# Combining a block's last tiles on VectorE in aligned pairs, with gate and base operations 1024 columns wide

## The chip, the cores and the metric

The kernel runs on one core of one Trainium2 chip, in float32. The metric is the device time of one execution in microseconds; lower is better.

## The reference, cut to what matters

The block is an adaLN transformer layer: a first half (RWKV-like time and channel mixing) gives `x4`, and a second half is a mixture of experts on it. What the change touches is the last sum:

```
h   = layernorm(x4) * (1 + cb) + sb
out = x4 + gb * (shared(h) + sum over the top 2 of 16 experts of gate_e * expert_e(h))
```

`x4` is 4 batches of 512 tokens with 512 channels. In the kernel that is 16 tiles of 128 tokens by 512 channels, tiles 0 to 3 being batch 0 and so on. `gb` is one row of 512 numbers per batch.

## The kernel before, in words

The routed experts are computed on tokens sorted by expert: a loop over pairs of slots of 128 tokens on TensorE, ScalarE and VectorE, whose results SP stores in `ys_s` in HBM. It ends about 875 us into the span. This document is about the 55 us behind it.

**What the work behind the loop is.** For each of the 16 tiles the final sum is put together in `g1b[:, t]` in SBUF:

1. GpSimd gathers the tile's rows of `ys_s`, first those of the lower expert into `g1b` (line 2567), then those of the upper into `g2b` (line 2574). These are indirect DMAs; the row numbers are in `spos` in SBUF. The order is: lower 0 to 9, upper 0 to 7, lower 10 to 15, a wait for the first up-projection of batch 3 (`s_up`), upper 8 to 15. The gather of an upper tile t from 8 on also waits until t - 7 tiles are counted in `s_o4`.
2. ScalarE scales `g1b[:, t]` by the lower gate (`scaled`, line 2350).
3. VectorE adds the upper part times its gate (`upper_row`, line 1939).
4. From tile 8 on, the shared expert's down-projection lies in PSUM, and VectorE adds it (`shared_row`, line 1944) and counts `s_gsh`.
5. VectorE multiplies by `gb` (`gated`, line 1948).
6. Tiles 0 to 7 and 12 to 15: VectorE adds a base, `base8` or `bsb` (`based`, line 1954), and counts `s_o4`; SP waits for each tile's count in turn and stores it to the output (line 853). Tiles 8 to 11 have no base operation: `s_o4` is counted behind the gate, and GpSimd adds them onto the output with an accumulating DMA (line 2597), where `x4` lies already.

**What runs beside it.** TensorE computes the shared expert for batches 2 and 3 in parts of 128 mid-channels, 4 to a batch. The up-projection of part n (8 to 11 for batch 2, 12 to 15 for batch 3) writes `up_ps[n % 2]`; ScalarE applies Gelu (line 2290) and copies the high part out (line 2298); VectorE subtracts it to get the low part (`mid_lo(n)`, line 1743). The up-projection of part n waits for `mid_lo(n - 2)`, which frees the bank. The down-projections take `mid_lo` of all four parts. `ht_lo(3, ...)` (line 1737) makes the low parts of batch 3's input.

**What sets the order.** Each engine's order is written out by hand. On VectorE it is the list at the end of its program: `mid_lo` and `ht_lo` calls with `combine` calls between them. `combine` takes a list of one or two tiles and does each step for all of them before the next step; an operation waits (`s_dve` or `s_gsh`) only for the one of its own tile, so that in a pair the other tile's operation runs between the two.

Of the kernel before, what the change touches and what calls it, by code (L numbers as in the profile page):

```python
# [17 lines left out]
ALU = mybir.AluOpType  # L18
# [3 lines left out]
P = 128  # L22
H = 512
# [3 lines left out]
TT = T // P  # L27
# [14 lines left out]
SB = 2  # L42
ERING = RING - BASE
NG = 8
LATE = (NB - 1) * TT
# [21 lines left out]
def adaln_block(nc, x_d, c_d, wmod_d, vecs_d, wtm_d, wcm_d, wrt_d, wex_d, out_d):  # L67
    top = ExitStack()
    with top:
        def sem(name):  # L70
            return top.enter_context(nc.semaphore(name))

        def sbuf(stack, name, shape, dt=F32):
            return stack.enter_context(nc.sbuf_tensor(name, shape, dt))
# [109 lines left out]
        g1b = sbuf(overlay, "g1b", [P, NT, H])  # L184
# [11 lines left out]
        bsb = sbuf(overlay, "bsb", [P, NT - LATE, H])  # L196
# [26 lines left out]
        base8 = sbuf(ph3, "base8", [P, SB * TT, H])  # L223
# [12 lines left out]
        now = sbuf(ph3, "now", [P, NE])  # L236
# [26 lines left out]
        gb2 = sbuf(ph4, "gb2", [P, NB, H])  # L263
# [61 lines left out]
        s_dve = sem("s_dve")  # L325
# [10 lines left out]
        s_gsh = sem("s_gsh")  # L336
# [31 lines left out]
        s_o4 = sem("s_o4")  # L368
# [97 lines left out]
        def gathered(t):  # L466

            i = t % NG
            before = 32 * NB if i < TT else 0 if i < TT + 2 else 16 * (NE - PRE) // 2
            return before + 16 * (t // NG + 1)  # L470
# [13 lines left out]
        def dn_of(t):  # L484
            return dn_ps[t % 4] if t < SB * TT else dn5_ps[(t - SB * TT) % 6]
# [777 lines left out]
        def _(dve):  # L1263
            own = Count(s_dve)
# [433 lines left out]
            for g in range(NB * MF):  # L1698
                b, m = divmod(g, MF)
                t = (b - 1) * TT  # L1700
# [30 lines left out]
            def ht_lo(b, tiles):  # L1731
                if 0 in tiles:
                    dve.wait_ge(s_htlo, b * KT)
                hi, lo = (ht_of(b)[:, i] for i in range(2))
                for k in tiles:
                    dve.wait_ge(s_hthi, b * KT + k + 1)
                    dve.tensor_tensor(lo[:, k, :], lo[:, k, :].bitcast(F32), hi[:, k, :].bitcast(F32), ALU.subtract)\
                        .then_inc(s_htlo, 1)

            def mid_lo(n):  # L1740
                b, m = divmod(n, KT)
                dve.wait_ge(s_midhi, n + 1)
                dve.tensor_tensor(mid_of(b)[:, 1, m, :], up_ps[n % 2][:, :], mid_of(b)[:, 0, m, :].bitcast(F32),
                                  ALU.subtract).then_inc(s_midlo, 1)
# [101 lines left out]
            t = NT - TT  # L1846
# [87 lines left out]
            def upper_row(t):  # L1934
                dve.wait_ge(s_o1, t + 1)
                dve.wait_ge(s_gat[t % NG], gathered(t))
                if t == 0:
                    dve.wait_ge(s_gates, 1)
                return own.up(dve.scalar_tensor_tensor(out=g1b[:, t], in0=g2b[:, t], scalar=gates[:, 1, t:t + 1],
                                                       in1=g1b[:, t], op0=ALU.mult, op1=ALU.add))  # L1940

            def shared_row(t):
                dve.wait_ge(s_dn, t + 1)
                dve.tensor_tensor(g1b[:, t], dn_of(t)[:, :], g1b[:, t], ALU.add).then_inc(s_gsh, 1)

            def gated(t):
                dve.wait_ge(s_bsl, 16 * (NT - LATE + NB))
                return dve.tensor_tensor(g1b[:, t], g1b[:, t], gb2[:, t // TT], ALU.mult)

            def based(t):  # L1950
                if t == 0:
                    dve.wait_ge(s_base, 16 * SB * TT)
                base = base8[:, t] if t < SB * TT else bsb[:, t - LATE]
                dve.tensor_tensor(g1b[:, t], g1b[:, t], base, ALU.add).then_inc(s_o4, 1)

            def combine(tiles, middle=()):
                now = {}
                for t in tiles:
                    now[t] = upper_row(t)
                for n in middle:  # L1960
                    mid_lo(n)
                if tiles[0] >= SB * TT:
                    for t in tiles:
                        dve.wait_ge(s_dve, now[t])
                        shared_row(t)
                for t in tiles:
                    if t >= SB * TT:
                        dve.wait_ge(s_gsh, t + 1)
                    else:
                        dve.wait_ge(s_dve, now[t])  # L1970
                    if SB * TT <= t < LATE:
                        gated(t).then_inc(s_o4, 1)
                        del now[t]
                        continue
                    now[t] = own.up(gated(t))
                for t in tiles:
                    if t in now:
                        dve.wait_ge(s_dve, now[t])
                        based(t)

            mid_lo(8)
            mid_lo(9)
            combine([0])
            mid_lo(10)
            ht_lo(3, [0, 1])
            mid_lo(11)
            ht_lo(3, [2, 3])
            combine([1, 2])
            combine([3, 4])
            combine([5, 6])  # L1990
            mid_lo(12)
            combine([7])
            mid_lo(13)
            combine([8, 9], middle=[14])
            mid_lo(15)
            combine([10, 11])
            combine([12, 13])
            combine([14, 15])

        @block.scalar  # L2000
        def _(act):
# [635 lines left out]
```

## Time and profile before

| what | value |
|---|---|
| runs of the kernel | 936.26 us median of 3 (936.14 to 937.33) |
| the profiled execution | 932.21 us, span 930.4 us |
| granted TensorE clock, mean | 0.99 of full |
| TensorE busy over the span | 887.3 us (95%) |
| VectorE busy over the span | 523.6 us (56%) |
| ScalarE, GpSimd busy | 383.0 us (41%), 387.1 us (42%) |

The span is what the trace covers of the execution. Durations in the rows come from this one execution; `xN` is the number of instructions in a group, and an arrow `<-` behind an idle time names what ended it.

### The profile page before, as it was taken

Reading aid. Unit: us, or ns where it says so; the run is one execution under the profiler, and the core shown is the slowest. Engines: PE = TensorE matmul, PEld = TensorE weight load, DVE = VectorE, ACT = ScalarE, POOL = GpSimd, SP = SyncE. Lnnn points to the kernel's source line nnn. Section 1 sums busy time; section 2 is a strip of 40 time slices with the busy share of each in tenths; the row PEclk is TensorE's granted clock in tenths of the full one; section 3 lists DMA queues with packets and bytes.
Section 4 is the critical chain, followed back from the end, with each engine's and each line's share of the span. In section 5 each row is a group of like instructions: output and inputs, shape, how many; then the busy total and the mean of one; then the engine's idle time right before and its main releaser. Section 6 shows DMA issues by size and latency. Waiting matters only on the chain.

```text
span 930.4 us, 13567 instructions
## 1 busy us (share of the span) xinstructions
PE 887.3 (95%) x4264; PEld 714.8 (77%) x4265; DVE 523.6 (56%) x999; ACT 383.0 (41%) x632; POOL 387.1 (42%) x282
## 2 busy tenths in 40 slices
PE   6899879999998999999999999999999999999995
PEld 2467658878776888888888888888887888878874
DVE  5798797998667111263226522651496444444388
ACT  2666565583735533322232223225443333333252
POOL 3331200100022546316301630268537699888584
PEclk9999989999999999999999999999999999999998
DMA  9657578566056327487213421466435789786787
GB/s 354 214 150 230 198 234 264 162 201 215 1 171 218 131 93 237 145 261 260 91 35 129 143 91 35 137 216 225 159 115 183 243 259 275 270 270 204 248 245 173
DMA packets 121824, 174.03 MB, mean 187 GB/s; under 512 B 8216, under 2 KB 69656, under 8 KB 118704
## 3 DMA queue, kind: packets, MB, share of 16 engines
q1 hardware_dynamic: 58896, 111.55, 35.4%
q0 software_dynamic: 9216, 34.61, 12.1%
q10 hardware_dynamic: 53664, 27.26, 10.4%
q8 instruction: 27, 0.44, 0.2%
q14 instruction: 21, 0.17, 0.1%
HBM read 97.58 MB, written 75.81 MB: 186 GB/s over the span
## 4 chain that ended last, share of the span: by engine, by line
PE 76%; DVE 7%; DMA 5%; POOL 4%; issue 4%; ACT 2%; SPq 0%; DVEq 0%; ACTq 0%; POOLq 0%
PE kk_ps L426 6%; PE kv_ps L426 6%; PE kk_ps L428 6%; PE kv_ps L428 6%; PE kk_ps L427 6%; PE kv_ps L427 6%; PE mm_ps L426 6%; PE mm_ps L428 6%; PE mm_ps L427 6%; PE up_ps L426 3%; POOL g1b L2567 2%; DMA xsb<-xs_s 2%; PE up_ps L427 2%; PE up_ps L428 2%; PE dn_ps L428 2%
## 5 line engine op out<-in xcount | busy, mean ns | idle before, releaser
L1569 DVE TENSOR_TENSOR silu<-kk_ps,silu 128x512 fp32r<-128x512 f32 x64 | 44.3, 692 | 198.5 <-ACT silu L2238 197.9
L2234 ACT ACTIVATE kk_ps<-kk_ps 128x512 f32<-128x512 f32 x64 | 37.2, 582 | 207.2 <-PE kk_ps L428 207.2
L426 PE MATMUL kk_ps<-xk,cm_w 128*128 128x512 f32 x256 | 100.8, 394 | 0.0
L426 PE MATMUL kv_ps<-cm_w,silu 128*128 128x512 f32 x256 | 100.5, 393 | 0.0
L428 PE MATMUL kk_ps<-xk,cm_w 128*128 128x512 f32 x256 | 99.8, 390 | 0.0
L428 PE MATMUL kv_ps<-cm_w,silu 128*128 128x512 f32 x256 | 99.7, 390 | 0.0
L427 PE MATMUL kk_ps<-xk,cm_w 128*128 128x512 f32 x256 | 99.6, 389 | 0.0
L427 PE MATMUL kv_ps<-cm_w,silu 128*128 128x512 f32 x256 | 99.6, 389 | 0.0
L2404 POOL TENSOR_TENSOR cm_w<-stage,cm_w 128x1024 fp32r<-128x1024 f32 x16 | 38.7, 2426 | 88.3 <-ACT cm_w L2019 72.5
L1896 DVE TENSOR_TENSOR xsT<-xs_ps,xsT 128x512 fp32r<-128x512 f32 x42 | 29.1, 692 | 75.7 <-ACT xsT L2321 75.6
L2411 POOL TENSOR_TENSOR rs<-mv,neghalf 128x4 f32<-128x4 f32 (+2 forms) x13 | 13.5, 1039 | 133.8 <-DVE mv L1279 133.7
L2462 POOL TENSOR_TENSOR rs<-mv,neghalf 128x1 f32<-128x1 f32 x16 | 16.1, 1009 | 126.4 <-DVE mv L1594 126.4
L2047 ACT ACTIVATE mix<-raw_ps 128x512 fp32r<-128x512 f32 x64 | 37.4, 594 | 56.7 <-DVE raw_ps L1350 54.0
L426 PE MATMUL mm_ps<-mix,wkv_w 128*128 128x512 f32 x128 | 52.4, 409 | 5.0 <-DVE x2b L1391 4.1
L428 PEld LDWEIGHTS kv_ps<-cm_w,silu 128*128 128x128 f32 x256 | 48.1, 188 | 10.2
L428 PEld LDWEIGHTS kk_ps<-xk,cm_w 128*128 128x128 f32 x256 | 48.0, 188 | 10.2
L427 PEld LDWEIGHTS kv_ps<-cm_w,silu 128*128 128x128 f32 x256 | 48.1, 188 | 9.8
L427 PEld LDWEIGHTS kk_ps<-xk,cm_w 128*128 128x128 f32 x256 | 48.1, 188 | 9.7
L426 PEld LDWEIGHTS kv_ps<-cm_w,silu 128*128 128x128 f32 x256 | 48.1, 188 | 9.7
L426 PEld LDWEIGHTS kk_ps<-xk,cm_w 128*128 128x128 f32 x256 | 48.1, 188 | 9.6
L1350 DVE SCALAR_TENSOR_TENSOR raw_ps<-dT,vecs,hT 128x512 f32<-128x512 f32 x64 | 49.9, 796 | 3.0
L427 PE MATMUL mm_ps<-mix,wkv_w 128*128 128x512 f32 x128 | 50.6, 396 | 0.0
(298 smaller groups left out, 2338.5 us busy)
## 6 DMA issues: line engine op xcount, KB each, us to landing
xs_s<-zero ACTq DMA_DIRECT2D x13, 1024.0 KB, 6.2
ys_s<-zero ACTq DMA_DIRECT2D x13, 1024.0 KB, 6.4
xsb<-xs_s SPq DMA_DIRECT2D x44, 256.0 KB, 3.4
ys_s<-ysb SPq DMA_DIRECT2D x41, 256.0 KB, 3.6
ex_raw<-in_wex POOLq DMA_DIRECT2D x9, 1024.0 KB, 6.7
stage<-in_wcm SPq DMA_DIRECT2D x16, 512.0 KB, 4.0
wmod<-in_wmod SPq DMA_DIRECT2D x6, 1024.0 KB, 12.2
ex_raw<-in_wex SPq DMA_DIRECT2D x6, 1024.0 KB, 7.7
```

The costliest lines, as they stand in the source:

```text
L426: pe.matmul(out, lhs[0], rhs[0], start=first, stop=False)
L427: pe.matmul(out, lhs[0], rhs[1], start=False, stop=False)
L428: return pe.matmul(out, lhs[1], rhs[0], start=False, stop=last)
L1350: dve.scalar_tensor_tensor(out=out, in0=dT[:, k, :], scalar=vecs[:, vec, k:k + 1], in1=hT[:, k, 0:T], op0=ALU.mult, op1=ALU.add).then_inc( ...
L1569: dve.tensor_tensor(silu[:, g % NSILU, 1, :], kk_ps[g % 2][:, :], silu[:, g % NSILU, 0, :].bitcast(F32), ALU.subtract).then_inc(s_silo, 1)
L1896: dve.tensor_tensor(xsT[:, par, 1], xs_ps[par][:, :, :], xsT[:, par, 0].bitcast(F32), ALU.subtract)\
L2047: act.activation(mix[:, i % 2, 0, k, :], raw_at(s, b, k), ACT.Copy)\
L2234: act.activation(kk_ps[g % 2][:, :], kk_ps[g % 2][:, :], ACT.Silu).then_inc(s_silu, 1)
L2404: pool.tensor_tensor(w[:, 1, k0:k0 + KT // 2, :], stage[:, n % 2].rearrange("p (k c) -> p k c", c=H), w[:, 0, k0:k0 + KT // 2, :].bitcast( ...
L2411: pool.tensor_tensor(rs[:, j0:j1].rearrange("p (t a) -> p t a", a=1), mv[:, j0:j1, 1:2], neghalf[:, :].rearrange("p (t a) -> p t a", a=1). ...
L2462: pool.tensor_tensor(rs5[:, t % 2:t % 2 + 1], mv5[:, t % 2, 1:2], neghalf[:, :], ALU.pow)\
L2567: pool.indirect_dma_start(g1b[:, t], None, ys_s, bass.IndirectOffsetOnAxis(ap=spos[:, 0, t:t + 1], axis=0))\
```

## The change

Four edits, all in VectorE's program. `combine(t)` now takes an even tile number and treats tiles t and t + 1. `gated` and `based` work on both tiles in one instruction of 1024 columns, the gate row being read twice by a broadcast. They can start only when the operations before them are through for both tiles, and they count `s_o4` by 2 at once. `shared_row` and `upper_row` stay one instruction per tile. The pairs are 0-1, 2-3, ... 14-15 in place of 0, 1-2, 3-4, 5-6, 7, 8-9, ...: tile 0, which stood between `mid_lo(9)` and `mid_lo(10)`, moves behind `mid_lo(11)` and `ht_lo(3, [2, 3])`, and tile 7 stands before `mid_lo(13)` together with tile 6.

```diff
             def gated(t):
                 dve.wait_ge(s_bsl, 16 * (NT - LATE + NB))
-                return dve.tensor_tensor(g1b[:, t], g1b[:, t], gb2[:, t // TT], ALU.mult)
+                b = t // TT
+                return dve.tensor_tensor(g1b[:, t:t + 2], g1b[:, t:t + 2],
+                                         gb2[:, b:b + 1].to_broadcast([P, 2, H]), ALU.mult)
 
             def based(t):
                 if t == 0:
                     dve.wait_ge(s_base, 16 * SB * TT)
-                base = base8[:, t] if t < SB * TT else bsb[:, t - LATE]
-                dve.tensor_tensor(g1b[:, t], g1b[:, t], base, ALU.add).then_inc(s_o4, 1)
-
-            def combine(tiles, middle=()):
-                now = {}
-                for t in tiles:
-                    now[t] = upper_row(t)
+                base = base8[:, t:t + 2] if t < SB * TT else bsb[:, t - LATE:t - LATE + 2]
+                dve.tensor_tensor(g1b[:, t:t + 2], g1b[:, t:t + 2], base, ALU.add).then_inc(s_o4, 2)
+
+            def combine(t, middle=()):
+
+                now = [upper_row(t), upper_row(t + 1)]
                 for n in middle:
                     mid_lo(n)
-                if tiles[0] >= SB * TT:
-                    for t in tiles:
-                        dve.wait_ge(s_dve, now[t])
-                        shared_row(t)
-                for t in tiles:
-                    if t >= SB * TT:
-                        dve.wait_ge(s_gsh, t + 1)
-                    else:
-                        dve.wait_ge(s_dve, now[t])
-                    if SB * TT <= t < LATE:
-                        gated(t).then_inc(s_o4, 1)
-                        del now[t]
-                        continue
-                    now[t] = own.up(gated(t))
-                for t in tiles:
-                    if t in now:
-                        dve.wait_ge(s_dve, now[t])
-                        based(t)
+                if t >= SB * TT:
+                    for i in range(2):
+                        dve.wait_ge(s_dve, now[i])
+                        shared_row(t + i)
+                    dve.wait_ge(s_gsh, t + 2)
+                else:
+                    dve.wait_ge(s_dve, now[1])
+                if SB * TT <= t < LATE:
+                    gated(t).then_inc(s_o4, 2)
+                else:
+                    dve.wait_ge(s_dve, own.up(gated(t)))
+                    based(t)
 
             mid_lo(8)
             mid_lo(9)
-            combine([0])
             mid_lo(10)
             ht_lo(3, [0, 1])
             mid_lo(11)
             ht_lo(3, [2, 3])
-            combine([1, 2])
-            combine([3, 4])
-            combine([5, 6])
+            combine(0)
+            combine(2)
+            combine(4)
             mid_lo(12)
-            combine([7])
+            combine(6)
             mid_lo(13)
-            combine([8, 9], middle=[14])
+            combine(8, middle=[14])
             mid_lo(15)
-            combine([10, 11])
-            combine([12, 13])
-            combine([14, 15])
+            combine(10)
+            combine(12)
+            combine(14)
```

## Rows read from the trace of the kernel before

**Rows 1.** Chain that ended last, 860 to 931 us: start us, us, what

```profile
900.00 3.43 POOL g1b L2567
...
903.73 0.96 POOL g2b L2574
...
905.00 4.91 DMA g2b<-ys_s,spos
```

**Rows 2.** VectorE in order of time, first tile and first pair: start us, us, engine, line

```profile
884.73 0.75 DVE L1939 SCALAR_TENSOR_TENSOR g1b<-g2b,gates,g1b 128x512 f32<-128x512 f32 x1 [3.31 <-DMA g2b<-ys_s,spos]
885.51 0.69 DVE L1948 TENSOR_TENSOR g1b<-g1b,gb 128x512 f32<-128x512 f32 x1
886.24 0.69 DVE L1954 TENSOR_TENSOR g1b<-g1b,base 128x512 f32<-128x512 f32 x1
886.85 0.68 DVE L1743 TENSOR_TENSOR mid<-up_ps,mid 128x512 fp32r<-128x512 f32 x1
...
891.31 1.41 DVE L1939 SCALAR_TENSOR_TENSOR g1b<-g2b,gates,g1b 128x512 f32<-128x512 f32 x2
892.63 1.29 DVE L1948 TENSOR_TENSOR g1b<-g1b,gb 128x512 f32<-128x512 f32 x2
893.84 1.29 DVE L1954 TENSOR_TENSOR g1b<-g1b,base 128x512 f32<-128x512 f32 x2
895.04 1.41 DVE L1939 SCALAR_TENSOR_TENSOR g1b<-g2b,gates,g1b 128x512 f32<-128x512 f32 x2
```

**Rows 3.** VectorE in order of time, the middle of the stretch

```profile
902.51 0.69 DVE L1743 TENSOR_TENSOR ht<-up_ps,ht 128x512 fp32r<-128x512 f32 x1
...
905.23 0.68 DVE L1743 TENSOR_TENSOR ht<-up_ps,ht 128x512 fp32r<-128x512 f32 x1
907.86 0.75 DVE L1939 SCALAR_TENSOR_TENSOR g1b<-g2b,gates,g1b 128x512 f32<-128x512 f32 x1 [1.94 <-DMA g2b<-ys_s,spos]
910.00 0.75 DVE L1939 SCALAR_TENSOR_TENSOR g1b<-g2b,gates,g1b 128x512 f32<-128x512 f32 x1 [1.39 <-DMA g2b<-ys_s,spos]
910.67 0.68 DVE L1743 TENSOR_TENSOR ht<-up_ps,ht 128x512 fp32r<-128x512 f32 x1
```

**Rows 4.** VectorE in order of time, the last three pairs

```profile
914.27 1.41 DVE L1939 SCALAR_TENSOR_TENSOR g1b<-g2b,gates,g1b 128x512 f32<-128x512 f32 x2
...
917.99 1.41 DVE L1939 SCALAR_TENSOR_TENSOR g1b<-g2b,gates,g1b 128x512 f32<-128x512 f32 x2
...
926.64 1.29 DVE L1954 TENSOR_TENSOR g1b<-g1b,bsb 128x512 f32<-128x512 f32 x2
```

**Rows 5.** GpSimd in order of time, two of the lower gathers

```profile
893.86 1.50 POOL L2567 DMA_INDIRECT g1b<-ys_s,spos  x1 [0.30 <-issue]
...
896.93 2.76 POOL L2567 DMA_INDIRECT g1b<-ys_s,spos  x1 [0.30 <-issue]
```

**Rows 6.** VectorE groups by line, two widths: xcount | busy us, mean ns | idle before

```profile
L1896 DVE TENSOR_TENSOR xsT<-xs_ps,xsT 128x512 fp32r<-128x512 f32 x42 | 29.1, 692 | 75.7 <-ACT xsT L2321 75.6
...
L1901 DVE TENSOR_TENSOR mbT<-tm_ps,mbT 128x256 fp32r<-128x256 f32 x41 | 17.2, 419 | 0.2 <-DVE base L1755 0.2
```

**Rows 7.** ScalarE in order of time, the last batch's activations

```profile
900.26 0.58 ACT L2290 ACTIVATE up_ps<-up_ps 128x512 f32<-128x512 f32 x1 [5.89 <-PE up_ps L428]
...
906.35 0.58 ACT L2290 ACTIVATE up_ps<-up_ps 128x512 f32<-128x512 f32 x1 [2.16 <-PE up_ps L428]
```

**Rows 8.** TensorE in order of time, first product of an up-projection tile

```profile
903.25 0.50 PE L426 MATMUL up_ps<-mid,ex_w 128*128 128x512 f32 x1 [0.31 <-DVE ht L1743]
```

**Rows 9.** Busy time by stretch: us, PE, PEld, DVE, ACT, POOL, clock, DMA share, GB/s

```profile
922.00:924.00 2.00, 0.00 (x0) 0.00 (x0) 2.00 (x4) 0.00 (x0) 0.00 (x0) 1.00 0.93 217
```

**Rows 10.** SP's queue in order of time, two loads issued back to back

```profile
567.92 0.92 SPq L629 DMA_DIRECT2D xkr<-xk_s  x2
```

**Rows 11.** Line 853, SP's output stores: issue ns, first and last start, landing

```profile
L853 SPq DMA_DIRECT2D out<-g1b x12: 332/332/342, 887.0 to 928.0; - x12
...
DMA to landing us min/median/max: 2.0/2.6/4.8
```

## The prediction, made before the changed kernel was run

> **What bounds the kernel now.** I read the chain of waits first, from its end. The reader is to see that behind the experts' loop it runs along GpSimd's queue of gathers, through one lower gather of 3.43 us, into the upper gathers of tiles 8 and 9, the second of which lands 4.91 us after its issue [rows 1]. Then I read VectorE in order of time. It works without a gap from 891.31 to about 905.9, then stands 1.94 us for tile 8's gather and 1.39 us for tile 9's [rows 3], 3.33 us in all, and from 910.00 runs without a gap to 926.64 + 1.29 = 927.93 us [rows 4]. TensorE has nothing left from 922 us on [rows 9], so it does not set the end. After VectorE only the store of tile 15 is left: it is issued at 928.0 and takes at least 2.0 us to land [rows 11], and the span ends at 930.4. So what counts is when VectorE's last operation ends.
>
> **Part 1, tile 0 moves.** Its three operations and the start of part 10 take 884.73 to 886.85 = 2.12 us, in a stretch where VectorE otherwise idles (3.31 us before it) [rows 2]. They move behind 891.31, into the gapless run: 2.12 us more before the waits for tiles 8 and 9. The low part of part 10 can start only 0.1 us sooner, as ScalarE's copy is its other input; nothing gained there. SP's store of tile 0 goes with it, from 887 to about 895 us; nothing but other stores stands behind it in SP's queue. No gather waits for tile 0 so early: the first, tile 8's, starts at 903.73.
>
> **Part 2, two operations become one.** Two independent 512-column operations of one line are 893.84 - 892.63 = 1.21 us apart [rows 2], 0.60 each. The trace has no 1024-column operation on VectorE. From below I bound it by the slope between 256 and 512 columns: 692 - 419 = 273 ns [rows 6], so 692 + 546 = 1.24 us long and 0.60 + 0.55 = 1.15 us to the next independent start; from above by 1.21, no gain at all. I take 1.15, as the slope is of the same kind of instruction. By the Trainium skill ("VectorE: DVE Perf Modes", section on the TRN2 errata) an fp32 tensor_tensor takes (N + 151) / 0.96 ns, 1224 ns at 1024; over 14 operations that would make the sum 0.2 us smaller.
>
> **Part 3, the waits inside a pair.** An operation that waits for the one just before it starts 886.24 - 885.51 = 0.73 us after it, against 0.60: 0.13 us of latency, and 0.78 behind an upper operation, against 0.66 [rows 2]. In the old pairs the other tile's operation covered this. Now the gate waits for the second upper or shared operation, and the base for the whole gate. So, start to start:
> - pairs of tiles 0 to 7: 0.66 + 0.78 + (0.73 + 0.55) + 1.15 = 3.87 us, before 895.04 - 891.31 = 3.73 [rows 2];
> - a pair with a shared part and no base (8, 10): 1.32 + 0.60 + 0.73 + 1.15 = 3.80 us, before 917.99 - 914.27 = 3.72 [rows 4];
> - a pair with both (12, 14): 1.32 + 0.60 + 0.73 + 1.28 + 1.15 = 5.08 us, before (927.93 - 917.99) / 2 less the last one's tail of 0.04 = 4.93 [rows 4].
> By itself the pairing costs 0.14, 0.08 and 0.15 us a pair; the wide operation does not pay for its wait.
>
> **Part 4, the gathers.** A gather on GpSimd normally takes 0.96 us [rows 1], but some take 1.50, 2.76 and 3.43 [rows 1, 5]. Lined up with VectorE by what they take over 0.96: the one at 893.86 seems held until 894.40, 0.56 us after a base of two SBUF inputs began [rows 2]; the one at 896.93 until 898.73, 0.04 before the next pair begins (895.04 + 3.73); the one at 900.00 until 902.47, 0.04 before a low part, which has a PSUM input [rows 3]. So a gather that starts beside gates and bases waits until one ends, and can miss the gap of about 0.05 us to the next, several times in a row. After the change the gap before each gate and each base is some 0.13 us wider, by part 3. I take it that a gather gets in there, so that one wide operation at most holds it: 1.1 us. Lined up so, the six lower gathers end at about 899 to 901 us, not 903.43. The upper gathers then wait for the first up-projection of batch 3, which ScalarE sees at 900.26 [rows 7], so tile 8's starts between 900.3 and 901.5 and tile 9's by 903.0, landing by 908. The Trainium skill ("SBUF — State Buffer", section "Who interferes with whom") says that a VectorE instruction with two SBUF inputs contends with a GpSimd instruction that reads SBUF, and that the second one waits for the whole of the first. The rows agree for these gathers; that it speaks against wider operations is a rival below.
>
> **The sum.** From 891.31, three pairs: 891.31 + 3 x 3.87 = 902.92; part 12's low part 903.52; pair 6: 907.39, so part 13 starts there and not at 905.23 [rows 3]; 907.99 tiles 8 and 9, now ready: 909.31; part 14: 909.91; shared 0.60 + 0.73: 911.24; gate: 912.39. Part 15's low part needs TensorE, which waits for part 13's: 907.39 + 0.69 = 908.1. From a held start at 903.25 [rows 8] ScalarE's Gelu followed at 906.35 [rows 7], 3.10 us; the low part comes two activations later, 0.62 + 0.63: 908.1 + 3.10 + 1.25 = 912.45, so a wait of 0.06. Then 913.05, pair 10: 916.85, pair 12: 921.93, pair 14 with its tail of 0.09: 927.10, against 927.93: 0.83 us less. In short: the waits for tiles 8 and 9 go, 3.53 us from start to start (891.31 + 3 x 3.73 + 2.12 + 1.20 + 1.32 = 907.14 would be part 14's start, and it is 910.67); tiles 0 to 7 take 4 x 3.87 = 15.48 us in the run in place of 13.31, so 2.17 more; 2 x 0.08 + 2 x 0.15 + 0.06 are paid behind: 0.83 left.
> At the end both stores of the last pair are released together. Before, tile 14's went 0.6 us ahead. Two issues on SP take 0.92 us, 0.46 each [rows 10], so tile 15's goes 0.46 us later than it could: 0.83 - 0.46 = **0.4 us faster**. The profiled execution's 932.21 becomes 931.8; the median stands 4.05 us above it, so 935.9.
> What hides the rest: TensorE's part 15 comes 2 us later, but its last down-projection, with 0.6 us of this passed on, is done by 922.6, and its reader stands at about 923.9. If that cover went, TensorE would add up to 1 us. GpSimd's accumulating stores of tiles 10 and 11 start where pair 10's gate ends, 0.3 us earlier.
>
> **The rivals.** 0.2% is 1.9 us, about what a measurement of this kernel can tell from no change.
> - *A, forecast, 0.48*: 935.9.
> - *B, gathers as late as before, 0.27*: GpSimd still misses gaps. Tile 9's gather lands at 909.9 and its operation starts at 910.00. The end gains nothing and pays 2 x 0.08 + 2 x 0.15 + 0.46: +0.9 us, 937.2. For it: the 2.76 and 3.43. Against it: gaps about three times as wide.
> - *C, slower, 0.11*: the hold grows. Gathers get in only where a run of two-SBUF operations ends. Pair 6 now runs from 903.5 to 907.4, right over tile 8's and 9's gathers, where before only tile 7 stood. If tile 8's starts at 903.73 and is held to 907.2, it needs 0.96 us more and some 3 to land, 911.2, and tile 9's follows 1.3 us later at 912.5: 2.5 us later than 910.0, and 0.9 paid: 939.7. It decides from the point where tile 9's gather lands after 911. By the Trainium skill's rule above a hold is one instruction, here 1.24 us; it takes a run of them to reach this price.
> - *D, faster, 0.07*: the 0.13 us waits are not there for wide operations. Thirteen of them lie on the way, two in each pair from 0 to 6 (part 15 moves with them) and five behind part 15; 13 x 0.13 = 1.7 us: 934.2.
> - *E, it does not do what it says, 0.07*: the broadcast read makes the gate slower than two operations (up to 2 x 0.69 = 1.38 us, 0.23 more, eight times: +1.8), or the time moves for reasons outside of this stretch: 934 to 938.
>
> **How the numbers follow.** The likeliest is A. A and B hold 0.75; C lies above and D below. From 934.5 to 937.8 takes in A, B, the bound of no gain per wide operation (14 x 0.06 = 0.8 us) and most of E. Faster by over 1.9 us (below 934.4): D and a part of E, 0.10. Slower by over 1.9 us (above 938.1): C and a little of E, 0.13. Within: 0.77.
>
> **What would show it.** Wide gates and bases of 1.22 to 1.24 us; 1.27 us from a gate to its base; no idle time on VectorE before tiles 8 and 9; lower gathers 13 to 15 under 2.1 us each; tile 8's upper gather at 900.3 to 901.5; VectorE's end near 927.1 and two stores 0.46 us apart. A wait for tile 9's gather of over 1 us proves A wrong; a wide operation over 1.3 us proves part 2 wrong; a last TensorE product after 923 proves the cover wrong.

## The result, and the profile after

The changed kernel takes 942.52 us (median of 6, 940.69 to 947.66), the kernel before 936.80 in the same session (median of 6, 935.05 to 941.43). The ratio is 1.006, 95% interval 1.0037 to 1.0083: slower, by 5.7 us between the medians. The forecast of 935.9 and its range up to 937.8 both missed. In a later session one execution of a version below took 1785.94 us and one of the kernel before 1457.24; the ratios leave them out.

The profiled execution took 942.66 us, its span is 940.9. VectorE in order of time, from the copy that frees the loop's last bank to the end of the run of pairs (start us, us, engine, line, what; in brackets the idle time before and what ended it):

```profile
885.73 0.69 DVE L1909 COPY ysb<-dn_ps 128x512 f32<-128x512 f32 x1 [5.03 <-remote]
...
896.97 1.41 DVE L1939 SCALAR_TENSOR_TENSOR g1b<-g2b,gates,g1b 128x512 f32<-128x512 f32 x2
898.41 1.22 DVE L1949 TENSOR_TENSOR g1b<-g1b,gb 128x1024 f32<-128x1024 f32 x1
899.72 1.23 DVE L1956 TENSOR_TENSOR g1b<-g1b,base 128x1024 f32<-128x1024 f32 x1
900.87 1.41 DVE L1939 SCALAR_TENSOR_TENSOR g1b<-g2b,gates,g1b 128x512 f32<-128x512 f32 x2
...
907.55 1.23 DVE L1956 TENSOR_TENSOR g1b<-g1b,base 128x1024 f32<-128x1024 f32 x1
913.43 0.69 DVE L1743 TENSOR_TENSOR ht<-up_ps,ht 128x512 fp32r<-128x512 f32 x1 [4.66 <-ACT ht L2292]
...
923.63 1.41 DVE L1939 SCALAR_TENSOR_TENSOR g1b<-g2b,gates,g1b 128x512 f32<-128x512 f32 x2
...
927.47 1.41 DVE L1939 SCALAR_TENSOR_TENSOR g1b<-g2b,gates,g1b 128x512 f32<-128x512 f32 x2
...
932.59 1.41 DVE L1939 SCALAR_TENSOR_TENSOR g1b<-g2b,gates,g1b 128x512 f32<-128x512 f32 x2
...
936.56 1.23 DVE L1956 TENSOR_TENSOR g1b<-g1b,bsb 128x1024 f32<-128x1024 f32 x1
```

Everything that VectorE does by itself came as worked out: wide operations of 1.22 to 1.23 us, 1.31 us from a gate to its base (forecast 1.28), 3.90 us for a pair of tiles 0 to 7 (3.87), 3.84 for pair 10 (3.80), 5.12 for pair 12 (5.08). The waits for tiles 8 and 9 of [rows 3] are gone. In their place stands one wait, 4.66 us, for part 12's low part, which the forecast had without a wait.

GpSimd, lower gathers from tile 10 on and the first upper one:

```profile
899.51 0.96 POOL L2561 DMA_INDIRECT g1b<-ys_s,spos  x1 [0.30 <-issue]
900.78 1.00 POOL L2561 DMA_INDIRECT g1b<-ys_s,spos  x1 [0.30 <-issue]
...
906.01 1.01 POOL L2561 DMA_INDIRECT g1b<-ys_s,spos  x1 [0.32 <-issue]
912.42 0.96 POOL L2568 DMA_INDIRECT g2b<-ys_s,spos  x1 [5.40 <-PE up_ps L428]
```

None is held now, against 1.50, 2.76 and 3.43 us [rows 1, 5]. But tile 8's upper gather waits 5.40 us, for the same thing as VectorE: part 12's up-projection. TensorE and ScalarE there:

```profile
904.50 0.39 PE L426 MATMUL up_ps<-mid,ex_w 128*128 128x512 f32 x1
904.84 0.40 PE L427 MATMUL up_ps<-mid,ex_w 128*128 128x512 f32 x1
906.97 0.39 PE L428 MATMUL up_ps<-mid,ex_w 128*128 128x512 f32 x1 [1.73 <-issue]
908.40 0.39 PE L426 MATMUL up_ps<-mid,ex_w 128*128 128x512 f32 x1 [1.05 <-issue]
...
910.67 0.63 PE L426 MATMUL up_ps<-mid,ex_w 128*128 128x512 f32 x1
...
911.52 0.63 PE L428 MATMUL up_ps<-mid,ex_w 128*128 128x512 f32 x1
```

```profile
912.19 0.58 ACT L2284 ACTIVATE up_ps<-up_ps 128x512 f32<-128x512 f32 x1 [12.15 <-PE up_ps L428]
```

TensorE stands between products of part 12's one up-projection, for 1.73, 1.05 and, before the next product, 0.32 us, waiting for nothing that the profile shows ("issue"). Behind this half-idle stretch the granted clock is lower (mean 0.60 over 909 to 913 us, so partly at 1.2 GHz, with products 0.43 us apart in place of 0.23). Twelve products 0.23 us apart from 904.50 would end at about 907.4; they end at 911.52 + 0.63 = 912.15. By an estimate from these rows, 3.7 of the 4.8 us are the stops and 1.1 the lower clock. ScalarE starts at once behind them, so in this trace VectorE's 4.66 us are TensorE's own lateness. The first row of VectorE above, its 5.03 us of idle time at the loop's exit, is not in the trace read for the forecast, but it is no work of the change: the kernel before shows it too, as the first experiment tells.

### The profile page after: what moved, and what is told of

It is laid out like the page before. It is cut to its first block, busy times and chain, and to the rows that moved or that the text cites. A ratio compares the mean times of both kernels' runs of the same rounds, so it can differ in the third digit from the quotient of the medians.

```text
span 940.9 us, 13550 instructions
## 1 busy us (share of the span) xinstructions
PE 893.0 (95%) x4264; PEld 718.3 (76%) x4265; DVE 523.8 (56%) x985; ACT 382.8 (41%) x632; POOL 381.9 (41%) x282
## 4 chain that ended last, share of the span: by engine, by line
PE 79%; DVE 8%; DMA 5%; issue 4%; ACT 3%; SPq 1%; POOL 1%; DVEq 0%; ACTq 0%
PE kk_ps L426 6%; PE kv_ps L426 6%; PE kk_ps L428 6%; PE kv_ps L428 6%; PE kk_ps L427 6%; PE kv_ps L427 6%; PE up_ps L426 4%; PE mm_ps L426 4%; PE mm_ps L427 4%; PE mm_ps L428 4%; PE up_ps L428 4%; PE up_ps L427 3%; PE dn_ps L426 3%; PE dn_ps L428 3%; PE dn_ps L427 3%
## 5 line engine op out<-in xcount | busy, mean ns | idle before, releaser
L428 PEld LDWEIGHTS kk_ps<-xk,cm_w 128*128 128x128 f32 x256 | 48.0, 188 | 10.2
```

The source lines that it names most:

```text
L428: return pe.matmul(out, lhs[1], rhs[0], start=False, stop=last)
```

## The experiments

Fourteen runs were made, of ten new kernels and four repeats. One number serves for all traces: the **run**, from the start of the first pair's upper operations (896.97 here) to the end of VectorE's last operation (936.56 + 1.23). For each trace I take VectorE's waits of 0.36 us or more in it off; the rest is work. (In the old order tile 0's operations stand ahead of the run, in the new one inside it.) The column "trace" is the time of the profiled execution. Ratios are to runs of the kernel before on the same chip. (These rows are worked out from VectorE's rows in order of time.)

```
kernel                        ratio  [95%]             run    waits   work   trace
before, as forecast from      -                        36.62   3.33   33.29   932.21
before, again                 1.0018 [0.9999, 1.0037]  34.57   1.18   33.39   936.45
wide 8-15, old order          1.0029 [1.0009, 1.0050]  35.36   1.33   34.03   935.80
wide all, old order           1.0029 [1.0010, 1.0049]  36.93   2.42   34.51   938.26
before, pauses                1.0028 [1.0011, 1.0046]  40.76   7.45   33.31   945.79
before, exit paused           1.0070 [1.0042, 1.0099]  39.81   6.44   33.37   940.50
new order, 512 wide           1.0044 [1.0026, 1.0062]  41.08   6.07   35.01   941.57
new order, 512 wide, again    1.0054 [1.0033, 1.0075]  40.29   5.25   35.04   941.09
after                         1.0060 [1.0037, 1.0083]  40.82   4.66   36.16   942.66
after, again                  1.0056 [1.0034, 1.0079]  43.87   7.47   36.40   943.73
after, stores late            1.0057 [1.0033, 1.0081]  43.10   6.88   36.22   941.12
after, gathers "spaced"       1.0051 [1.0029, 1.0072]  43.09   6.79   36.30   946.04
after, part 13 inside         1.0051 [1.0033, 1.0068]  40.85   4.75   36.10   940.96
after, pauses                 1.0018 [0.9995, 1.0040]  37.67   1.56   36.11   933.46
after, pauses + part 13       0.9981 [0.9959, 1.0003]  37.41   1.42   35.99   933.41
after, pauses + part 13 again 1.0016 [0.9995, 1.0037]  37.76   1.68   36.08   939.99
```

The control, text for text the kernel before, came out at 1.0018, and one text measured twice at 0.9981 and 1.0016. So differences below about 0.3% are not read. A trace is one execution: those of "before, pauses" and of the "spaced" version are the slowest of their twelve, those of "after, pauses" and of "wide 8-15" the fastest.

**Both kernels again.** No edit.

> The kernel before, unchanged, for a second trace and as a control of the comparison. Both theories: ratio 1.000 +- 0.002. Theory I: no issue stall of TensorE over 1 us between the loop's exit and the end, its last program fetch lies 1.5 us or more ahead of the product that needs it. Theory D: stalls of this kind show here too in some executions.

> The changed kernel once more. In its first trace VectorE's own operations behaved as forecast, and the time was lost in two places that the change does not touch: around the loop's exit (876 to 886 us) and where TensorE stood 1.7 + 1.0 + 0.3 us for instructions at 905 to 909 us, just as the last 16 KB piece of its program was fetched (906.0 us, against 895.8 before). Theory I (code fetch): the stall at TensorE's last fetch belongs to the changed kernel and comes back, with the product before it held 2 us or more; the ratio stays near 1.006 (1.004 to 1.008). Theory D (a disturbed trace): the lost time around the exit is chance of the loop and its transfers; the trace shows neither stall, and the ratio lies within 0.998 to 1.003.

Measured: 936.87 and 942.03 us. The difference is real and repeats. Neither theory on the stop of TensorE comes true as it stands. In the changed kernel's first trace the one 16 KB packet of the instruction queue in this stretch starts at 906.01 us and takes 0.91, and TensorE goes on at 906.97; that fits the first stop and not the two behind it. In the second trace the packet starts at 900.93, no product is held near it, and the ratio is the same. The kernel before's second trace is the more useful one. VectorE at the loop's exit, at tile 0, at the first pair, at part 12's low part and at tiles 8 and 9:

```profile
885.00 0.69 DVE L1909 COPY ysb<-dn_ps 128x512 f32<-128x512 f32 x1 [5.01 <-remote]
...
891.75 0.75 DVE L1939 SCALAR_TENSOR_TENSOR g1b<-g2b,gates,g1b 128x512 f32<-128x512 f32 x1 [3.72 <-DMA g2b<-ys_s,spos]
...
897.60 1.40 DVE L1939 SCALAR_TENSOR_TENSOR g1b<-g2b,gates,g1b 128x512 f32<-128x512 f32 x2
...
909.74 0.69 DVE L1743 TENSOR_TENSOR ht<-up_ps,ht 128x512 fp32r<-128x512 f32 x1 [0.74 <-issue]
...
913.59 1.42 DVE L1939 SCALAR_TENSOR_TENSOR g1b<-g2b,gates,g1b 128x512 f32<-128x512 f32 x2 [0.44 <-DMA g2b<-ys_s,spos]
```

Its six lower gathers take 0.96 us each, the first and the last of them:

```profile
898.88 0.96 POOL L2567 DMA_INDIRECT g1b<-ys_s,spos  x1 [0.30 <-issue]
...
905.21 0.96 POOL L2567 DMA_INDIRECT g1b<-ys_s,spos  x1 [0.30 <-issue]
```

Nothing holds them, and the wait for tiles 8 and 9 is 0.44 us, not 3.33. The exit's idle time, 5 to 6 us, stands in 12 of the 16 traces of the table, of either order. That the exit costs 5 us and the gathers are unheld in the one, and the reverse in the other, is how these two executions of one kernel differ (the trace of "before, pauses" has both); the forecast was made from the second kind, whose 932.21 us lie 4 us under the median.

In the changed kernel's second trace, TensorE is not late but its counts are:

```profile
910.79 0.39 PE L428 MATMUL up_ps<-mid,ex_w 128*128 128x512 f32 x1
917.34 0.80 PE L426 MATMUL up_ps<-mid,ex_w 128*128 128x512 f32 x1 [6.17 <-issue]
```

```profile
915.35 0.58 ACT L2284 ACTIVATE up_ps<-up_ps 128x512 f32<-128x512 f32 x1 [7.97 <-remote]
...
918.99 0.58 ACT L2284 ACTIVATE up_ps<-up_ps 128x512 f32<-128x512 f32 x1 [2.43 <-remote]
```

Part 13's last product ends at 908.2 and part 14's at 911.2; ScalarE, which has nothing else to do there, starts at 915.35 and 918.99, 7.2 and 7.8 us later. VectorE's low part of part 13 follows at 916.60, after 4.58 us of waiting, and TensorE's part 15 at 917.34: its 6.17 us, put down to "issue", are the wait for that low part.

**Order and width apart.** The pairs of the new order with operations of 512 columns, measured in two sessions; and the reverse, wide operations in the old order:

```diff
-            combine([0])
...
+            combine([0, 1])
+            combine([2, 3])
+            combine([4, 5])
             mid_lo(12)
-            combine([7])
+            combine([6, 7])
```

> Only the order of the change: tile 0 behind the low part 11, pairs 0-1 to 14-15, but every gate and base 512 columns wide and waiting for its own tile alone, as before. If the order does it (tile 0's move and both stores of a pair together beside TensorE's fetch and the gathers), the time is that of the changed kernel, 1.004 to 1.008 of before. If it is the wide operations, 0.998 to 1.001: by the sum made before, the order alone gives VectorE's end 0.3 to 1.0 us back.

> The order of the change with operations of 512 columns, a second time, for another trace. Its first trace had three gathers held 2.77, 3.42 and 3.43 us in a row, tile 8's upper gather issued 16.2 us behind the first pair (12.4 in the kernel before), and VectorE waiting 5.61 us for it. Theory H (hold): this comes again, three holds of over 2.5 us, a wait of over 4.5 us, ratio 1.003 to 1.006. Else the wait is under 3.5 us and the slowness has another place.

```diff
-            combine([8, 9], middle=[14])
+            combine_w(8, middle=[14])
...
-            combine([10, 11])
-            combine([12, 13])
-            combine([14, 15])
+            combine_w(10)
+            combine_w(12)
+            combine_w(14)
```

(`combine_w` is the changed kernel's `combine`; the second version has it for 1-2, 3-4 and 5-6 as well.)

> Only the wide operations, and only in the pairs that both kernels have (8-9, 10-11, 12-13, 14-15); tiles 0 to 7 in the old order and width. By the terms of the prediction: 2 x 0.08 + 2 x 0.15 for the waits and 0.46 for the late store, so 0.9 us slower, ratio 1.001. If the wide operations cause the loss by the program's length (6 VectorE instructions fewer) or in another way, 1.004 or more; if the order does, 1.001 or less.

> The wide operations everywhere (pairs 1-2, 3-4, 5-6, 8-9 and on), but tile 0 early and tile 7 alone as in the kernel before, so the order is the old one. If the wide operations free the gathers and that costs, the stall is here too: ratio 1.003 to 1.006. If it is tile 0's move and the pairing of the stores by two more tiles, 1.000 to 1.002 (prediction's terms: 3 x 0.14 + 0.9 us).

Measured: order alone 1.0044 and 1.0054, width alone 1.0029 twice. The order carries most of the loss; whether width costs anything stays open (both intervals lie above 1, but the control's 1.0018 is as near). With 512-wide operations in the new order ScalarE starts parts 12 to 14 within 0.1 us of each end, but GpSimd is held:

```profile
898.10 2.77 POOL L2573 DMA_INDIRECT g2b<-ys_s,spos  x1 [0.30 <-issue]
901.17 3.42 POOL L2566 DMA_INDIRECT g1b<-ys_s,spos  x1 [0.30 <-issue]
904.90 3.43 POOL L2566 DMA_INDIRECT g1b<-ys_s,spos  x1 [0.30 <-issue]
```

and VectorE pays for it at tile 8:

```profile
918.71 1.42 DVE L1939 SCALAR_TENSOR_TENSOR g1b<-g2b,gates,g1b 128x512 f32<-128x512 f32 x2 [5.61 <-DMA g2b<-ys_s,spos]
```

That is rival C's mechanism, held gathers in a longer run of pairs. C was priced at 3.4 us; the two ratios are 4.1 and 5.1 us. In the changed kernel the wide operations' waits do let the gathers in, as part 4 said; its loss has the same size by another way.

**Stores out of the way.** SP keeps tiles 0 to 7 back until eight are counted.

```diff
-                sp.wait_ge(s_o4, t + 1)
+                sp.wait_ge(s_o4, max(t + 1, SB * TT))
```

> The changed kernel, but SP stores tiles 0 to 7 only once all eight are counted (about 12 us later for the first). Theory S (saturation): once VectorE no longer holds the gathers, 14 to 22 of them run without a gap beside the pairs' stores, together 340 to 380 KB a us for 8 us, and in that stretch counts and instructions of the engines come late (TensorE's product held 3.5 and 6.2 us in the two traces, ScalarE 8 us behind TensorE's count). Without the stores in that stretch the stall shrinks under 1.5 us and the time falls by 2 to 5 us, ratio 0.999 to 1.003. Theory G: the gathers alone do it (there is a like stall at the loop's exit): unchanged, 1.004 or more.

Measured 943.6 us, 1.0057. ScalarE still starts parts 13 and 14 3.7 and 8.1 us late (ends 906.34 and 909.05):

```profile
910.04 0.58 ACT L2284 ACTIVATE up_ps<-up_ps 128x512 f32<-128x512 f32 x1 [5.17 <-PE up_ps L428]
...
917.15 0.58 ACT L2284 ACTIVATE up_ps<-up_ps 128x512 f32<-128x512 f32 x1 [5.90 <-remote]
```

No store is issued before 909.53, so the first lateness has none beside it, and the loss is what it was: the stores are not needed for it. Of the second this can't be said, as the held stores go out then.

**Gathers spaced.** Two waits for `s_o4` (2 and 4) before lower gathers 12 and 14.

> The changed kernel, but GpSimd issues the lower gathers 12 and 14 only when 2 and 4 tiles are counted, which puts gaps of 1 to 2 us where VectorE's holds had put them before. Theory S and theory G both: the stall behind the first pair shrinks under 1.5 us, ratio 0.999 to 1.003. A rival, that the time is lost by the wide operations or the order themselves: 1.005 as before.

Measured 941.46 us, 1.0051. The counts were already there when GpSimd came to the waits, so nothing was spaced and the trace is that of the changed kernel: ScalarE 6.5 and 7.8 us late (ends 911.26, 914.25; starts 917.77, 922.05). As a test of the gathers it is void; it is one more measurement of the changed kernel.

**Gathers paused,** with waits that hold:

```diff
             for t in range(SOON, NT):
+                if t == SOON + 3:
+                    pool.wait_ge(s_o4, 4)
                 gather_lower(t)
             pool.wait_ge(s_up, (NB - 1) * KT + 1)
+            pool.wait_ge(s_o4, 6)
```

> The changed kernel, but GpSimd waits for 4 counted tiles ahead of lower gather 13 and for 6 ahead of tile 8's upper gather, so that the 14 to 24 gathers in a row get two real pauses (the waits of f2_gathers_spaced were over before they were reached, so it spaced nothing). Theory G: in traces where over about 14 gathers ran without a pause TensorE's counts reached ScalarE late (7.1 and 7.8 us in e1_after_again, 3.7 and 8.0 in f1_stores_late); with the pauses each up-projection's count arrives within 0.5 us, VectorE has no wait over 1 us before part 12 and 13, and the ratio is 0.998 to 1.003. Theory O (order): the low part of part 13 behind a whole pair costs by itself: late counts or not, ratio 1.004 or more.

Measured 936.83 us, 1.0018: most of the loss is gone. The pause, and ScalarE on time:

```profile
899.08 1.22 POOL L2561 DMA_INDIRECT g1b<-ys_s,spos  x1 [3.35 <-DVE g1b L1956]
```

```profile
902.51 0.58 ACT L2284 ACTIVATE up_ps<-up_ps 128x512 f32<-128x512 f32 x1 [1.50 <-PE up_ps L428]
```

The end of each up-projection and ScalarE's start are within 0.1 us (902.5 and 902.51, 906.4 and 906.44). What is left is 1.56 us for tile 8's gather, and 1.50 us in which TensorE's part 15 waits for part 13's low part, which stands behind pair 6.

**Part 13's low part inside pair 6,** with the pauses, twice, and without them:

```diff
-            combine(6)
-            mid_lo(13)
+            combine(6, middle=[13])
```

> f5_gathers_paused, and the low part of part 13 in the middle of pair 6 instead of behind it, 2.5 us sooner, so that TensorE's part 15 isn't held. Theory O: TensorE's gap before part 15 (1.4 us at the least with the new order, none in the kernel before) goes, and the time falls by 1 to 3 us below f5. Theory G alone: within 0.5 us of f5, as TensorE has the slack; ratio 0.998 to 1.002.

> The changed kernel with both edits (two pauses in the gathers, part 13's low part inside pair 6), the same text as before, to narrow the interval: 934.2 to 935.5, 0.998 to 0.9995 of the kernel before if the gain is real; 1.000 to 1.001 if the first result was a lucky draw.

> The changed kernel with one edit: part 13's low part stands inside pair 6, behind its two upper operations, and no pause is put into GpSimd's gathers. Theory 'cover' (a low part behind a whole pair leaves TensorE's part 15 late; worth 1.9 to 2.6 us): 939 to 940.5, and with the late counts and the wait for part 12's low part left as they are, still 1.003 to 1.004 of the kernel before. Rival 'pauses' (the unbroken row of gathers is all of it): 941.5 to 942.5, 1.005 to 1.006, and ScalarE still starts part 13 over 3 us behind the end of its up-projection. If both are worth something, the two edits together (934.25 in an earlier run) minus the pauses alone (936.8) give 2.6 us for this edit, and the pauses the other 5.

Measured: 934.25 us (0.9981) and 939.48 us (1.0016) with the pauses, 940.96 us (1.0051) without. TensorE's gap before part 15 is gone in all three, but the time is not the better for it where the counts or issues are late: alone the edit gives nothing that can be told from the changed kernel. By the ratio that speaks for the expectation's rival, "pauses"; by the time it lies between the two, and that rival's sign, ScalarE over 3 us late at part 13, isn't in the trace. There TensorE stops within part 12 instead, as in the changed kernel's first trace:

```profile
905.72 0.49 PE L426 MATMUL up_ps<-mid,ex_w 128*128 128x512 f32 x1 [1.03 <-issue]
```

(The 16 KB packet of the instruction queue comes 3 us behind it, at 908.68.) In one session, with part 13 inside in both, the pauses bring the ratio from 1.0051 to 1.0016; the intervals just overlap. On top of the pauses its effect can't be told apart either, as the same text differs by as much from session to session. The second trace with the pauses has the loop exit's stall (4.99 us) and still a short run (37.76), so the pauses' effect on the run does not hang on that stall being absent.

**The kernel before, paused.** The same two pauses, at counts 5 and 7; and another, GpSimd waiting for the loop's end behind the fourth early gather, to keep the exit free.

> The kernel before with the two pauses alone (lower gather 13 behind tile 4's base, tile 8's upper gather behind tile 6's). If pauses help by themselves, whatever the pairing, then 934 to 935.5 (0.998 to 0.999), and the pairing would be worth nothing in the kernel with both edits. If they only mend what the change brings, 936 to 937.5 (0.9995 to 1.001): this kernel paused for 2.5 to 3.5 us by itself, and the later start of tile 8's upper gather (902.5 for 903.7) leaves the wait for tile 9's at its 1.4 us.

> The kernel before, but GpSimd pauses behind its fourth lower gather until the loop's last stores have landed. Its second trace had TensorE standing 2.8 us at the loop's exit and VectorE 5.0 us for the last slot, with 10 gathers in a row beside. Theory G (a long row of gathers makes counts and loop transfers late) : the exit has no gap over 1 us, the loop's last copy comes within 1 us of its product. The gathers end 4 to 6 us later themselves, so the time is about the same or some us worse, ratio 0.998 to 1.006. If the exit's gap stays at 2.8 us, it isn't the gathers.

Measured: 940.02 us (1.0028) and 941.07 us (1.007). Neither helps. In the first, three gathers in a row are held for 3.44, 3.43 and 3.42 us, and VectorE waits 6.85 us for ScalarE's scaled tile 8; the two pauses add nothing to that in this trace, since GpSimd reaches them late (0.30 us before each gather, as without them). So this trace, the slowest of its twelve, doesn't show a paused kernel at all, and the ratio can't be told from the control's. In the second the exit's stall is gone, but so it is in three other traces without this pause, which settles nothing. The later gathers cost: tile 0's operations wait 8.92 us and part 10's low part stands behind them, and in the run VectorE waits 2.18 us for part 12's low part and 4.26 for the gathers of tiles 8 and 9. So no gain from pauses is seen in the old order; in the new one they mend what it brings. No version was found that is measurably faster than the kernel before.

## Why the prediction was wrong

- **Parts 2 and 3, the cost of pairing: right.** The work of the run rose from 33.29 and 33.39 us to between 35.99 and 36.40, 2.6 to 3.1 more; the sum had 2.17 + 2 x 0.08 + 2 x 0.15 = 2.63. By the formula in the Trainium skill ("VectorE: DVE Perf Modes", section on the TRN2 errata) 1024 columns take 1.224 us, and the trace agrees with 1.22 to 1.23; the slope's 1.24 was 0.02 too long.
- **Part 1, tile 0: nearly right.** It cost its 2 us. "Nothing gained there" was wrong for executions in which tile 0's gather is late: there it held up part 10's low part. From the exit's copy to the first pair is 897.60 - 885.00 = 12.60 us before and 896.97 - 885.73 = 11.24 after, 1.36 less in these two traces.
- **Part 4, the gathers get in: right,** 0.96 to 1.02 us each. In none of the nine traces with wide operations on tiles 0 to 7 does one take over 1.78 us; with 512 columns one of 2.76 or more is in five of seven. But the kernel before can have them free too, and **what that was worth was wrong: the credit of 3.53 us** for the waits for tiles 8 and 9. In the kernel before's second trace these waits are 0.44 us. The forecast took the stall of one execution for the kernel's, though its own 4.05 us between that execution and the median said that it was not a usual one.
- **The sum's path through the low parts failed.** It runs from 902.92 to 903.52 and from 907.39 to 907.99 without a wait, so it takes it that ScalarE is done with parts 12 and 13 when VectorE comes to them, and books 0.06 us for part 15's. Part 12's low part waited 4.66 us; in the repeat the four low parts waited 0.59, 4.58, 1.63 and 0.67. No term stood for stops within TensorE's own work or for its counts being late. The sign given for this path failed with it: tile 8's upper gather starts 15.5 us behind the first pair, not 9.0 to 10.2. The cover that "What hides the rest" asks for, TensorE's last down-projection ahead of its reader, held by itself: the last product ends at 932.24 + 0.39 = 932.63 us and tile 15's shared operation starts at about 934.5.

```profile
932.24 0.39 PE L428 MATMUL dn_ps<-ex_w,ht 128*128 128x512 f32 x1
```

```profile
933.91 1.28 DVE L1944 TENSOR_TENSOR g1b<-dn_ps,g1b 128x512 f32<-128x512 f32 x2
```

- **In part 4, the rule that the gathers were said to agree with was read too widely.** In the Trainium skill ("SBUF — State Buffer", section "Who interferes with whom") a wait for the whole of one instruction is spelled out for VectorE's 2-port modes, and the same section has it that a tensor_tensor was not seen to stall a DMA. The rows here show gathers held beside such operations, and for more than one of them.

Together, from the exit's copy to VectorE's end, the second trace of before against the trace of after: 52.06 - 47.17 = 4.89 us, which is -1.36 in front of the run, +2.77 of work, +3.48 of waits (4.66 - 1.18). Behind VectorE's end the span goes on for 3.1 us, in both traces of before for 2.5: the two stores released together, 0.6 where 0.46 was forecast. With the pauses the same kernel has 1.4 to 1.7 us of waits, and comes out at 1.0018, 0.9981 and 1.0016: added work alone is 2.77 - 1.36 + 0.6 = 2.0 us, about what can be told from no change, and the waits make the rest. ("After, pauses" was read in its fastest execution; the 1.68 us of the repeat with part 13 inside are from a usual one.)

The forecast's rival C had the side right, with a chance of 0.11. Its mechanism is seen in the versions with 512 columns; in the changed kernel it was another one.

What is shown: the new order without pauses is slower in all seven measurements (1.0044 to 1.0060), with wide operations and without, and pauses that hold in GpSimd's gathers take most of it away there (three measurements). That only the new order loses isn't shown: wide operations in the old one lie at 1.0029 with intervals that overlap these, and the old order with the exit paused at 1.0070. What is only argued: that the moved tile 0 itself, by making room for more gathers side by side with part 12, is what calls the late counts. What is open: why counts and products come late.

## What to carry to other kernels

Before booking a stall as a gain, look for it in a second execution: here 3.3 us of waiting in one trace were 0.4 in the next, while the costs of the change were there in both. A term of nothing is a forecast too: where the sum lets one engine find another done (here VectorE and the low parts), ask what that engine's own time rests on. Moving such an operation forward need not pay: part 13's low part inside its pair closed TensorE's gap and gained no time that could be told. And when a change lets transfers run freer than before, test what that does to the rest, by a pause that is seen to hold in the trace; two of the pauses tried here held nothing, and only their traces told.

## What the runs showed of the hardware

**Counts and products come late beside a long row of gathers that nothing slows.** Eight of the 16 traces have 14 to 22 gathers one behind the other from the loop's exit on, none over 1.62 us and none paused. In each of them an up-projection's count is late at ScalarE or TensorE stops within the up-projection: by 1.3 us in the old order (three traces), by 3.7 to 8.1 us of late counts or 2.0 to 3.1 us of stops in the new one (five). In the other eight a gather of that row is held for 2.76 us or more, or a pause of 3.35 us stands in it, and ScalarE starts parts 12 to 14 within 0.1 us of their ends. The eight late ones all have the loop exit's stall, but so have four of the others, so the stall alone isn't it. (The split was found in the traces, not forecast.) What the DMA engines do beside it says less. Stretches of 5 us of the changed kernel's second trace (us, busy time of PE, PEld, DVE, ACT, POOL, granted clock, DMA share, GB/s):

```profile
897.00:902.00 5.00, 5.00 (x24) 4.14 (x23) 4.77 (x6) 1.06 (x2) 4.08 (x4) 1.00 0.70 190
902.00:907.00 5.00, 5.00 (x24) 4.14 (x23) 4.68 (x5) 0.80 (x2) 3.78 (x5) 1.00 0.92 293
907.00:912.00 5.00, 4.17 (x18) 2.81 (x16) 4.45 (x5) 0.38 (x1) 3.78 (x5) 1.00 1.01 365
912.00:917.00 5.00, 0.00 (x0) 0.00 (x0) 0.42 (x2) 1.18 (x2) 3.73 (x4) 0.92 0.94 311
```

and of the second trace with pauses and part 13 inside:

```profile
902.00:907.00 5.00, 5.00 (x24) 4.14 (x23) 4.83 (x7) 0.00 (x0) 1.41 (x2) 1.00 0.76 254
907.00:912.00 5.00, 5.00 (x24) 4.14 (x23) 4.22 (x6) 2.37 (x4) 4.02 (x4) 1.00 0.79 214
912.00:917.00 5.00, 5.00 (x24) 4.05 (x22) 3.90 (x5) 3.40 (x6) 4.08 (x4) 1.00 0.86 302
```

In the first, 22 gathers are issued without a pause and the share stays above 0.9 for 15 us; the counts come 7 to 8 us late, and TensorE stands idle behind them. In the trace of the changed kernel TensorE's own gaps (904.8 to 909) lie in a stretch with a share of 0.95 (904 to 909). The kernel before's second trace has 14 gathers in a row, shares of 0.93 and 0.97 over 901 to 911, and shows the mild form: ScalarE 1.3 us late once, one issue gap of 0.50 us. With the pauses, and with held gathers (0.72 over 907 to 912 in the new order with 512 columns), the counts come at once. Against full DMA engines as the cause speak two stretches. In the first trace with pauses the share is 0.91 over 905 to 910, with ScalarE on time. And in the version with late stores part 13's count is 3.7 us late at a share of 0.65:

```profile
906.30:910.00 3.70, 2.75 (x13) 1.94 (x11) 3.06 (x3) 0.00 (x0) 3.09 (x3) 1.00 0.65 176
```

So the lateness goes with the free row of gathers, and a high share isn't needed for it. How the row acts on counts and products is not shown. The profile itself lacks some of its own records (of landings) in the traces with an exit stall, about 7,000 to 7,200 of them against 7,838 in those without, so a part of the lateness could also be the profiler's. Every execution behind the medians has its span and clock on record as well, so the medians don't tell the two apart.

**A held gather moves with what VectorE runs.** Gathers beside runs of 512-column gates and bases are held in steps (1.50, 2.77, 3.43 us), beside 1024-column ones with their wider gaps 0.96 to 1.62 us, once 1.78. Where such a hold ends can be read off: all 13 gathers of 2.76 us or more are free again (by what they take over 0.96) 0.03 to 0.05 us before the operation behind the pair's last base starts, or could start. The first of the new order with 512 columns, above, is free at 898.10 + 2.77 - 0.96 = 899.91, and the next pair starts at

```profile
899.95 1.41 DVE L1939 SCALAR_TENSOR_TENSOR g1b<-g2b,gates,g1b 128x512 f32<-128x512 f32 x2
```

So a long hold lasts to the end of the run of gates and bases, four operations of 0.69 us; the two of 1.50 us beside bases end within it, just before the second base. Beside the wide gate the twelve gathers of 1.59 to 1.78 us are free 0.22 to 0.24 us before its base starts, so none is carried over into the base: 0.82 us at most, within one operation, as part 4 took it. But the same kernel's gathers were held in one trace and free in the next, so it also hangs on how the two engines happen to line up.
